# Filler matrix products in the edge stage of a two-layer graph network kernel

## The reference, cut

```python
w = jax.nn.silu(rbf @ We1 + be1) @ We2 + be2      # per edge: 64 -> 128 -> 128
m = w * (h[src] @ Wlin)                           # gathered row of the source node
agg = jax.ops.segment_sum(m, dst, num_segments=h.shape[0])
out = jax.nn.silu(agg @ Wn1 + bn1) @ Wn2 + bn2
return h + out
```

## Time and profile before

| | us |
|---|---|
| median of 3 runs | 4340.98 |
| lowest, highest run | 4338.73, 4369.01 |
| the profiled execution | 4300.25 |
| its span, first to last instruction | 4298.6 |
| the stretch 1550 to 4230 us, edge stage | 2680 |

### The profile page before, as it was taken

The page is one execution under the profiler, slowest core; times in us unless marked ns, Lnnn a source line. Parts: engine busy times, 40 slices in busy tenths (PEclk is TensorE's granted clock), DMA queues, the critical chain, the costliest instruction groups (busy, mean ns, idle before and its releaser), DMA issues.

```text
span 4298.6 us, 72566 instructions
## 1 busy us (share of the span) xinstructions
PE 3128.9 (73%) x20697; PEld 2292.9 (53%) x20698; DVE 2233.5 (52%) x5097; ACT 939.8 (22%) x2068; POOL 1497.9 (35%) x1601
## 2 busy tenths in 40 slices
PE   6979999999979956666666666666656566655656
PEld 5623566677759944444444444444445445444445
DVE  8999999888883433333333333333333333333333
ACT  4111344555541111111111111111111111111112
POOL 0000000000000045555555555555555565555541
PEclk8989999999989967777777777777777787777788
DMA  1000111222238932222222222222222222222211
GB/s 50 0 0 31 61 76 76 106 106 105 97 147 315 349 88 58 62 60 58 61 61 60 60 57 60 59 52 60 57 52 56 57 62 59 56 52 52 52 50 41
DMA packets 278886, 325.01 MB, mean 76 GB/s; under 512 B 231023, under 2 KB 238344, under 8 KB 266142
## 3 DMA queue, kind: packets, MB, share of 16 engines
q1 hardware_dynamic: 227518, 217.13, 15.2%
q0 software_dynamic: 51168, 106.07, 9.3%
HBM read 238.00 MB, written 85.09 MB: 75 GB/s over the span
## 4 chain that ended last, share of the span: by engine, by line
PE 34%; another core or an unknown queue 30%; DVE 17%; issue 14%; DVEq 4%; ACT 1%; ACTq 0%; DMA 0%; SPq 0%; POOL 0%; POOLq 0%
PE pc L1448 9%; DVE shared L1112 4%; PE pb L1430 4%; PE pc L1265 4%; PE pb L1271 3%; DVE shared L947 3%; PE pa L1271 3%; PE pd L1265 3%; PE pd L1229 2%; PE pa L1419 1%; DVE shared L1104 1%; DVE hch L947 1%; DVE dl_f L1111 1%; DVE c L947 1%
## 5 line engine op out<-in xcount | busy, mean ns | idle before, releaser
L481 POOL DMA_INDIRECT shared<-lin_table,idx x1568 | 1482.9, 946 | 1195.6 <-issue 464.6
L1448 PE MATMUL pc<-shared 128*128 128x128 f32 x3904 | 666.1, 337 | 790.7 <-DVE shared L1112 548.3
L1448 PEld LDWEIGHTS pc<-shared 128*128 128x128 f32 x3904 | 615.9, 246 | 843.6 <-DVE shared L1112 597.0
L1130 DVE TENSOR_TENSOR agg<-agg,pc 128x128 f32 x244 | 70.1, 287 | 1461.1 <-remote 1088.2
L713 ACT ACTIVATE shared<-pa,be_col 128x512 f32<-128x512 f32 x392 | 252.1, 684 | 2242.7 <-remote 1293.9
L1430 PE MATMUL pb<-we_sb,shared 128*128 128x128 f32 x3136 | 530.3, 316 | 116.0 <-issue 62.1
L1430 PEld LDWEIGHTS pb<-we_sb,shared 128*128 128x128 f32 x3136 | 443.8, 217 | 228.6 <-issue 154.9
L1112 DVE TENSOR_TENSOR shared<-pe_iota,dl_f 128x1024 f32<-128x1024 f32 x440 | 538.6, 1224 | 15.2
L510 POOL DMA_DIRECT2D lin_table<-c x12 | 9.3, 772 | 1525.7 <-issue 1336.0
L947 DVE TENSOR_SCALAR shared<-col_h,shared 128x784 bf16<-128x784 f16 x1092 | 401.6, 416 | 2.4 <-issue 2.0
L1104 DVE TENSOR_TENSOR shared<-pb,shared 128x512 f32<-128x512 f32 x392 | 255.3, 683 | 249.6 <-remote 205.2
(11 more groups left out here) (228 smaller groups left out, 3274.6 us busy)
## 6 DMA issues: line engine op xcount, KB each, us to landing
adjacency<-shared SPq DMA_DIRECT2D x49, 1568.0 KB, 5.6
shared<-adjacency SPq DMA_DIRECT2D x49, 1568.0 KB, 8.5
shared<-in_edge_attr_dram SPq DMA_DIRECT2D x195, 256.0 KB
shared<-lin_table,idx POOLq DMA_INDIRECT x1568
lin_table<-c POOLq DMA_DIRECT2D x12, 256.0 KB, 7.1
out_dram<-xr SPq DMA_DIRECT2D x12, 256.0 KB
shared<-in_dst_dram SPq DMA_DIRECT2D x1, 512.0 KB
shared<-in_src_dram SPq DMA_DIRECT2D x1, 512.0 KB
```

The costliest lines, as they stand in the source:

```text
L481: pool.indirect_dma_start(out=dest(s, j), out_offset=None, in_=table, in_offset=bass.IndirectOffsetOnAxis(ap=idx[:, s, j:j + 1], axis=0)). ...
L1448: last = pe.matmul(pc[:, 0:F], hot_f[:, 2 * i + h, :], msgs[s % 2][:, h, i, :], start=(h == 0 and i == 0), stop=(h == 1 and i == 3))
```

## The change

PE's loop gets two packets of four products each. Each product takes `zeros_b` as weights and 512 columns of `iota_u`, and writes the bank `pf`, which nothing in this stage reads. Nothing waits for them, and they wait for nothing. The first packet stands between `layer1` and `turn_ea`, the second behind `group_sums`.

```diff
+            def keep_busy(n):
+                for i in range(n):
+                    pe.matmul(pf[:, :], zeros_b[:, :], iota_u[:, :, :].rearrange("p d u -> p (d u)")[:, 0:512], start=True, stop=True)
...
                     layer2(g)
                     layer1(g + 1)
+                    keep_busy(4)
                     turn_ea(g + 2, it + ((s + 2) // RING + 1), (s + 2) % RING)
                     group_sums(g - 1, s - 1)
+                    keep_busy(4)
```

## The result

The change makes the kernel slower by 0.7%; over 20 runs each this is clear of zero, though a single run would hardly show it. I had forecast 6.9%.

The account below looks back on a forecast made before the run. The prediction took PE as the bound, working mainly while POOL's gathers stand still. Price 448 less cover 128 less clock 20 gave 300 us, so 4600 us for the profiled execution, 4641 us as median; range 4500 to 4850.

Parts of the forecast that it names:

- The wider one for 8 in 10: Range for the whole run's time, 4340 to 4950 us, leaving out the faster case and the far half of the slowest.
- What bounds the kernel: Edge stage: PE's completions come late while POOL gathers, so PE works mainly while POOL is stopped; stage 2680 us.
- Price of the products: 1536 products in PE's loop: 0.216 us each at full clock, 0.292 with 35% at half clock, 448 us in all.
- What they give back: PE's other rows, shortened by a higher clock: at most some 327 us, but products can't fill held stretches, so 20 us.
- what the profile would show: Signs in the edge stage: about 2980 us, clock 0.77 to 0.82, one-hot waits shorter by some 128 us, late completions not fewer or shorter.
- What hides them: PE's one-hot waits ahead of the sums: 55 of 103 take up both packets of the turn, 2.33 us each, 128 us.
- The sum: Whole run: 448 - 128 - 20 = 300 us added, giving 4641 us on the scale of the median, 6.9% more.
- Rival 4: Edge stage: cost and clock gain cancel, some 100 to 150 us back; 4298 to 4384 us, chance 0.10.
- Rival 2: Edge stage: products mostly hidden, only 24.7% of 448 = 111 us counts; 4452 us, chance 0.15.
- Rival 5: Held stretches of PE: one product in ten runs at 2.1 us, 323 us on top of the 300; 4964 us, chance 0.12.
- Rival 3: Behind a release: denser work raises PE's clock, 327 us come back, 4096 us; partly so 4100 to 4297 us, chance 0.13.

Follow-up runs that it names:

- g3: The kernel before with one gather per group instead of eight, on a chip with late completions: 3045.01 us, ratio 0.7077.
- g1: The kernel before with one gather per group instead of eight, on a chip where the kernel before takes 3553.04 us: 3043.58 us, ratio 0.8568.
- g4: The changed kernel, products included, with one gather per group instead of eight, on a chip with late completions: 3354.95 us, ratio 0.7797 against the kernel before.
- a_again: The changed kernel run once more without edits, beside the kernel before on one chip with late completions: 4355.99 us against 4299.99, ratio 1.0132.
- b_again: The kernel before run once more without edits, for a trace from a chip with late completions: 4301.66 us against 4299.99, ratio 1.0022.
- e4: The changed kernel with all eight products of 64 columns instead of 512: 4394.86 us, ratio 1.0167 against the kernel before.
- h1: The kernel before without the two bias products of layer2, on a chip where POOL gathers without a pause: 3552.99 us, ratio 1.0002.

## Why the prediction was wrong, point by point

Measured is 4368 us, outside the forecast's own range of 4500 to 4850. The wider one for 8 in 10, from 4340 us on, holds it, near its lower end.

**What bounds the kernel.** Right for the chips with late completions. That these come from the gathers was read from stretches in which the two coincide; g3 shows it by an experiment on such a chip. What I couldn't know is that they depend on the chip: on S and T the same program has none, and there my own figure of 1960 us for POOL is the stage. The forecast of 4641 us was for one kind of chip only, and on the other the answer is no change.

**Price of the products.** Nearly right. The price at full clock, 0.216 us each and 332 us in all, was measured as 310 us net where nothing hides it (g1 to g4), or 344 with the 34 us by which PE's other lines were less busy. For the clock I took 35% of them at half; the mean of 420 ns in a_again, between the 380 and 611 of the earlier trace rows, makes it 17%, so I estimate 0.216 x 1.17 x 1536 = 388 us, not 448.

**What they give back.** Too small. If the products cost 388 us and PE's busy time grew by 292, the other rows gave back 96 us, not 20. It can be checked without the estimate: the busy times of PE's five other lines, each taken alone, add up to 1801.7 us in b_again and 1707.4 in a_again, 94 less. The rows of the sums (337 to 317 ns) and of line 1430 (314 to 301) show it. Not all of it need be the clock, since in g4 the same sum fell by 34 us while the clock went only from 0.96 to 0.98. I had argued from one stretch, that a product can't fill the hole. That stretch is PE's wait for the one-hot matrix of a further block, and there indeed none can stand. But it is one kind of hole of two: the idle time ahead of first blocks was as large (365 against 350 us on Q), and the products filled it. The stage's clock rose, from 0.75 to 0.81, as I had said under what the profile would show (0.77 to 0.82). The rule of the Trainium skill ("TensorE: Matmul & The Clock Gate", section "Why this matters for your kernels"), that TensorE kept busy keeps its clock, agrees with this trace to that extent; it does not make the kernel faster.

**What hides them.** This is the step that failed most: "55 x 2.33 = 128 us". PE's idle time fell by 255 us. The split was right: ahead of further blocks the products hide nothing (350 and 339 us on Q). What was wrong is that a wait ahead of a first block could take up only the products of its own turn, 2.33 us. On Q 62 of these waits had the one-hot matrix as their releaser, 339 us in all; with the products 21 are left, 21 us in all. Each lost 5.1 us on average, twice what the products of one turn take. So the time of products in turns without a wait must have been taken up too: PE falls behind in them and waits less in a later turn. This last step is argued from the sizes; no run tests it by itself.

**The sum.** In place of 448 - 128 - 20 = 300 stands 388 - 255 - 96 = 37 us, the 37 us by which the stage grew between the two traces of Q (median of the runs there: 56 us). This sum must come out, since the 96 are 388 less the growth of PE's busy time; what is measured are the 292 and the 255. Of the 263 us between the two sums 60 are the price, 127 the cover and 76 the clock.

**The rivals.** Rival 4, that cost and gains cancel, is nearly what happened on the chips with late completions: it had 111 us exposed and 100 to 150 back, and by the sum above 388 - 255 = 133 are exposed and 96 come back. I gave it 0.10. Rival 2 had nearly the exposed part and no clock. Rival 5 is seen (products some 0.8 us apart near 3008 us) but doesn't decide: in a_again PE is idle for 34 us ahead of products, and the rival wanted 323. Rival 3 is ruled out: the clock gives back 96 us at most in eight products, far from 327.

**What stays open.** Why the total of the idle time fell in some kernels and not in others. It did so in the traces in which the clock rose (-255 us at 0.81, -270 at 0.85) and hardly in those in which it stayed (-8, -28 and -67 us at 0.74 to 0.76). Ahead of first blocks it is far below 365 us in all of them. The difference lies elsewhere: e4 is idle for 411 us ahead of further blocks and 305 ahead of `layer2`, a_again for 339 and 188. That the clock is the cause of this is not shown: products of 512 columns in both packets are what the two kernels with the large fall have in common as well, e4 and a_again ran on different chips, and the runs made to part the theories landed on chips without late completions. Nor is it shown why a single packet costs more than both; P and Q are different chips, and the change itself was not timed on P. And why PE's completions come late on some chips during gathers, and not on others, no run here tells; since each chip had one sitting, it may also be something of the sitting.

## What to carry to other kernels

- What filler work for the clock costs depends on the bound: its own time where its engine is the bound, nothing where another engine is. Price it once with the waits taken away (here: one gather instead of eight), and the rest of the sum is cover and clock.
- When you count the cover, sort the waits by whether the added work can delay the engine ahead of them at all (here first and further blocks), and then compare their total with the total of the added work. A cap by turn, as in my 55 x 2.33, came out at less than half.
- Time the kernel before beside every variant on the same chip. A ratio from one chip said +1.3%, from another 0.0%, and both were right.

## What the runs showed that I had not expected

- The same program took 4300 and 4331 us on two chips (and 4352 in the runs of the result) and 3553 us on three, with nothing between. The 750 us are in the edge stage: 2717 us on Q against the 1960 us of POOL's gathers.
- PE's completions come late, by 10 us and more, while POOL issues gathers, on some chips only. With one gather per group "remote" no longer releases DVE line 1130 or ACT line 713, and the two kinds of chip agree within 2 us (3043.6 and 3045.0).
- The cost did not grow steadily with the number of products: four cost 80 and 109 us and sixteen 182 on P, eight 56 on Q and 16 in the runs of the result.
- On T the bias products (h1 leaves out 392) and the filler together change PE's busy time in the stage by 296 us and the stage's clock from 0.85 to 0.94, and the time stays within 0.1%.
